# Bringing together the degrees' partial sums: two hops of small DMAs and a VectorE reduction in place of a TensorE matmul

## The reference

```
# layer 0: the same adj with x and with x2, an MLP of three ReLU layers on each
ax  = adj @ x          ; h = ax + (1 + eps) * ax ; 3 times: h = relu(h @ W[i].T + b[i])
x   = layernorm(x + concat(out1, out2) @ Wm.T + bm)
# layer 1: normalised by degrees
A_hat = adj + eye ; deg = sum(A_hat, axis=1) ; d = where(deg > 0, rsqrt(deg), 0)
x   = layernorm(x + (d[:, None] * A_hat * d[None, :] @ x) @ W.T + b)
```

## Time and profile before

| | |
|---|---|
| median of 3 runs | 594.1 us |
| the profiled execution | 593.58 us, of which span 591.8 us |
| TensorE matmul busy | 584.8 us (99%) |
| VectorE busy | 540.5 us (91%) |
| ScalarE busy | 372.2 us (63%) |
| GpSimd busy | 28.7 us (5%) |
| granted TensorE clock, mean | 0.997 |
| DMA, mean over the span | 239 GB/s |

### The profile page before, as it was taken

One profiled execution on the slowest core, in us unless ns is written; L12 is line 12 of the kernel. 1 busy time (PEld: TensorE's weight loads), 2 busy tenths in 40 slices (PEclk: granted clock), 3 DMA queues, 4 the chain that ended last, 5 costly groups with the idle time before them and its releaser, 6 DMA issues.

```text
span 591.8 us, 7721 instructions
## 1 busy us (share of the span) xinstructions
PE 584.8 (99%) x2676; PEld 484.3 (82%) x2676; DVE 540.5 (91%) x679; ACT 372.2 (63%) x494; POOL 28.7 (5%) x31
## 2 busy tenths in 40 slices
PE   8999999999999999999999999999999999999996
PEld 7888888888888888888888888867888888888885
DVE  6999999997988998998799999994899999989986
ACT  6554446842544773454667336486897888898893
POOL 1000000001100000110000020000200010010011
PEclk9999999999999999999999999999999999999998
DMA  9978565443554533354443375776699999999911
GB/s 334 370 271 296 202 226 197 142 148 137 214 205 170 190 145 142 142 213 174 181 150 138 138 293 189 286 299 212 245 353 413 364 370 383 400 365 374 387 42 71
DMA packets 27849, 141.56 MB, mean 239 GB/s; under 512 B 2608, under 2 KB 3376, under 8 KB 13616
## 3 DMA queue, kind: packets, MB, share of 16 engines
q1 hardware_dynamic: 27248, 139.54, 63.6%
q10 hardware_dynamic: 576, 1.70, 0.7%
HBM read 139.14 MB, written 2.10 MB: 239 GB/s over the span
## 4 chain that ended last, share of the span: by engine, by line
PE 98%; issue 0%; DVE 0%; POOL 0%; POOLq 0%; DVEq 0%
PE ps L468 81%; PE ps L544 7%; PE pd L486 6%; PE pd L497 2%; PE pd L530 1%; PE pd L592 1%; POOLq L118 0%; POOL rstd L1119 0%; DVE z L1090 0%; PE pd L494 0%; DVE stats L1095 0%; DVE outn L1104 0%; POOL identity L1123 0%; DVE mv L897 0%; DVEq L118 0%
## 5 line engine op out<-in xcount | busy, mean ns | idle before, releaser
L649 ACT ACTIVATE ahi<-raw 128x1024 fp32r<-128x1024 f32 x212 | 221.7, 1057 | 165.4 <-PE ps L468 152.8
L816 DVE TENSOR_TENSOR alo<-raw,ahi 128x1024 fp32r<-128x1024 f32 x212 | 257.2, 1220 | 29.7 <-ACT ahi L649 27.9
L468 PE MATMUL ps<-ahi,x2s 128*128 128x512 f32 x512 | 138.4, 389 | 0.0
L468 PE MATMUL ps<-ahi,x1hi 128*128 128x512 f32 x384 | 121.8, 393 | 0.0
L468 PE MATMUL ps<-alo,x1hi 128*128 128x512 f32 x384 | 120.5, 390 | 0.0
L468 PE MATMUL ps<-ahi,x1lo 128*128 128x512 f32 x384 | 120.4, 389 | 0.0
L468 PEld LDWEIGHTS ps<-ahi,x2s 128*128 128x128 f32 x512 | 96.1, 188 | 20.0
L468 PEld LDWEIGHTS ps<-ahi,x1hi 128*128 128x128 f32 x384 | 71.9, 188 | 15.9 <-issue 1.4
L468 PEld LDWEIGHTS ps<-alo,x1hi 128*128 128x128 f32 x384 | 72.0, 188 | 15.2 <-DVE alo L816 0.3
L468 PEld LDWEIGHTS ps<-ahi,x1lo 128*128 128x128 f32 x384 | 72.1, 188 | 14.9
L468 PE MATMUL ps<-alo,x2s 128*128 128x512 f32 x256 | 80.3, 389 | 0.0
(11 more groups left out here) (98 smaller groups left out, 510.7 us busy)
## 6 DMA issues: line engine op xcount, KB each, us to landing
raw<-a_t SPq DMA_DIRECT2D x108, 1024.0 KB, 4.9
raw<-a_t SPq DMA_DIRECT2D x32, 512.0 KB, 7.4
raw<-early SPq DMA_DIRECT2D x7, 512.0 KB, 7.8
xn<-x SPq DMA_DIRECT2D x3, 1024.0 KB, 8.1
out<-outn ACTq DMA_DIRECT2D x3, 512.0 KB, 6.7
par<-params SPq DMA_DIRECT2D x1, 708.0 KB, 12.8
raw<-head SPq DMA_DIRECT2D x2, 256.0 KB, 3.2
xn<-x SPq DMA_DIRECT2D x1, 512.0 KB, 7.2
```

Of the source, the lines that this page charges most:

```text
L468: mm = pe.matmul(ps[bank + (CH * (q % 2) if layer else 0)][:, :], block_of(w, n), a[c], start=(n == 0 and k == 0), stop=(n == JB - 1 and k ...
L649: act.activation(ring_hi(layer, q, n), raw_tile(layer, n), ACT.Copy).then_inc(hi_ready, 1)
L816: dve.tensor_tensor(ring_lo(layer, q, n), raw_tile(layer, n), as_f32(ring_hi(layer, q, n)), ALU.subtract).then_inc(lo_ready, 1)
```

## The change

`same_place`, `totals` and the matmul of `merge` go, with TensorE's waits for `partial_ready` and `deg_ready`. ScalarE gets two new steps in its order: `spread_partial` at n = 7 (plan 0) or 6 (plan 1) waits for `partial` and issues one DMA that writes it to DRAM (16 KB, 128 runs of 128 B); `gather_partial` two tiles later waits for that write and issues four DMAs that each read all four groups back to 32 partitions (16 KB, 128 runs of 128 B each). Both stand behind ScalarE's round of that tile and ahead of its ReLUs. VectorE's `degrees` waits for the four reads, adds the groups with one reduction and goes on as before, from SBUF.

```diff
--- before.py
+++ after.py
@@ -82,6 +82,7 @@
 DVE_AGGREGATE = (DVE_RESIDUAL[0] + 1 + KB // STATISTICS[0], DVE_RESIDUAL[1])
 DVE_DEGREES = tuple(k + 1 for k in DVE_RESIDUAL)
 DVE_TURN = (5, 4)
+ACT_SPREAD = (7, 6)
 DVE_BASE = 10
 DVE_BASE_LAST = 20
 DVE_SHIFT = tuple(k + 2 for k in DVE_AGGREGATE)
@@ -114,7 +115,7 @@
 X_AFTER = {1: 1, 3: 2, 6: 3, 12: 4, 20: 5}
 
 
-def build(nc, a_t, head, early, x12, params, out):
+def build(nc, a_t, head, early, x12, params, scratch, out):
     with ExitStack() as ctx:
         def sb(name, shape, dt=F32):
             return ctx.enter_context(nc.sbuf_tensor(name, shape, dt))
@@ -146,10 +147,11 @@
         hhi = sb("hhi", [P, M, CW], F32R)
         rowsum_all = sb("rowsum_all", [P, QW])
         partial = sb("partial", [P, QW // TB])
+        regrouped = sb("regrouped", [P, GROUPS, QW // TB])
+        together = sb("together", [P, QW // TB])
         own = sb("own", [P, QW // TB])
         degree = sb("degree", [P, KB])
         my_group = sb("my_group", [P, QW // TB])
-        same_place = sb("same_place", [P, P])
         xb = sb("xb", [P, KB, P])
         z = sb("z", [P, KB, P])
         par = sb("par", [P, PARAMS])
@@ -176,8 +178,6 @@
         merged = pd[:, 0:2, :].rearrange("p c (k d) -> p (c k) d", d=P)
 
         merged_last = lambda k: pd[:, 1 + max(k + 1 - TAIL[2][0], 0), (k % 4) * P:(k % 4 + 1) * P] if k >= HB else merged[:, k, :]
-        totals = pd[:, 2, 0:QW // TB]
-
         params_in = sem("params_in")
         x_in = [sem(f"x_in{i}") for i in range(len(X_PIECES))]
         x2_in = sem("x2_in")
@@ -206,6 +206,9 @@
         xb_ready = sem("xb_ready")
         turned_ready = sem("turned_ready")
         partial_ready = sem("partial_ready")
+        scratch_written = sem("scratch_written")
+        regrouped_in = sem("regrouped_in")
+        together_ready = sem("together_ready")
         own_ready = sem("own_ready")
         degree_ready = sem("degree_ready")
         deg_ready = sem("deg_ready")
@@ -490,8 +493,6 @@
             def merge(q):
 
                 wait(pe, h_ready, q * (4 * M) + 4 * M)
-                wait(pe, partial_ready, q + 1)
-                pe.matmul(totals, same_place[:, :], partial[:, :], start=True, stop=True, skip_group_check=True)
                 for k in range(KB):
                     for b in range(2):
                         mm = pe.matmul(merged[:, k, :], h[:, CH * b + k // 4, (k % 4) * P:(k % 4 + 1) * P],
@@ -505,7 +506,6 @@
                     if n == min(PE_DENSE[plan]):
                         wait(pe, raw_used, q * PAIRS + PAIRS)
                         wait(pe, z_ready, q)
-                        wait(pe, deg_ready, 2 * q)
                     dense(q, PE_DENSE[plan][n], plan)
                 if n == PE_MERGE[plan]:
                     merge(q)
@@ -684,6 +684,10 @@
             def mlp_step(q, n, plan):
                 if n == ACT_EVACUATE[plan]:
                     evacuate(q)
+                if n == ACT_SPREAD[plan]:
+                    spread_partial(q)
+                if n == ACT_SPREAD[plan] + 2:
+                    gather_partial(q)
                 if plan == 0 and n in (ACT_EVACUATE[0] + 1, ACT_EVACUATE[0] + 2):
                     for m in range(CH):
                         round_h(q, 0, CH * (n - ACT_EVACUATE[0] - 1) + m)
@@ -696,6 +700,18 @@
                     else:
                         to = lambda k: xn[:, bass.ds(q, 1), k * P:(k + 1) * P].rearrange("p o d -> p (o d)")
                     normalise(q + 1, to, xn_ready, range(size * (n - at), size * (n - at + 1)))
+
+            def spread_partial(q):
+
+                wait(act, partial_ready, q + 1)
+                act.dma_start(scratch, partial[:, :]).then_inc(scratch_written, 16)
+
+            def gather_partial(q):
+
+                wait(act, scratch_written, q * 16 + 16)
+                source = scratch.rearrange("(g r) b -> r g b", g=GROUPS)
+                for to in range(GROUPS):
+                    act.dma_start(regrouped[to * TB:(to + 1) * TB, :, :], source).then_inc(regrouped_in, 16)
 
             def round_y(g):
 
@@ -866,7 +882,11 @@
 
             def degrees(q):
 
-                dve.tensor_tensor(own[:, :], totals, my_group[:, :], ALU.mult).then_inc(own_ready, 1)
+                wait(dve, regrouped_in, (q + 1) * (16 * GROUPS))
+                dve.tensor_reduce(together[:, :], regrouped[:, :, :].rearrange("p g b -> p b g"),
+                                  mybir.AxisListType.X, ALU.add).then_inc(together_ready, 1)
+                wait(dve, together_ready, q + 1)
+                dve.tensor_tensor(own[:, :], together[:, :], my_group[:, :], ALU.mult).then_inc(own_ready, 1)
                 wait(dve, own_ready, q + 1)
                 dve.tensor_reduce(degree[:, :], own[:, :].rearrange("p (k g) -> p k g", g=GROUPS),
                                   mybir.AxisListType.X, ALU.add).then_inc(degree_ready, 1)
@@ -1124,14 +1144,8 @@
                                base=0, pattern=[[-1, P]], channel_multiplier=1).then_inc(warm_ready, 1)
             pool.wait_ge(warm_ready, 1)
             pool.memset(halves[:, :], -0.5).then_inc(const_ready, 2)
-            pool.memset(same_place[:, :], 0.0).then_inc(const_step, 1)
             pool.memset(my_group[:, :], 0.0).then_inc(const_step, 1)
-            pool.wait_ge(const_step, 3)
-            place = same_place[:, :].rearrange("p (g c) -> p g c", c=TB)
-            for g in range(GROUPS):
-                pool.affine_select(out=place, in_=place, compare_op=ALU.not_equal, fill=1.0, base=-TB * g,
-                                   pattern=[[0, GROUPS], [-1, TB]], channel_multiplier=1).then_inc(const_step, 1)
-                pool.wait_ge(const_step, g + 4)
+            pool.wait_ge(const_step, 2)
             of_group = my_group[:, :].rearrange("p (k g) -> p k g", g=GROUPS)
             for g in range(GROUPS):
                 pool.memset(of_group[g * TB:(g + 1) * TB, :, g], 1.0).then_inc(const_ready, 1)
@@ -1183,7 +1197,8 @@
     }
     nc = bacc.Bacc("TRN2", target_bir_lowering=False, num_devices=1)
     aps = [nc.dram_tensor(k, v.shape, F32, kind="ExternalInput").ap() for k, v in arrays.items()]
+    scratch = nc.dram_tensor("scratch", (P, QW // TB), F32).ap()
     out = nc.dram_tensor("out", (QUARTERS, P, QW), F32, kind="ExternalOutput").ap()
-    build(nc, *aps, out)
+    build(nc, *aps, scratch, out)
     r = run_bass_kernel_spmd(nc, [arrays], core_ids=[0])
     return r.results[0]["out"].reshape(_OUT)
```

## The result

| | before | changed |
|---|---|---|
| median of 5 runs each, us | 594.39 (594.02 to 594.75) | 603.17 (602.99 to 604.62) |
| ratio, 95% interval | | 1.0155 (1.0141 to 1.0169) |
| span of the profiled execution, us | 591.8 | 602.0 |
| mean granted clock | 0.997 | 0.996 |

The kernel became 8.8 us slower. 5.3 had been forecast, so the direction was right and the size was not: 603.2 lies above the range of 596.4 to 602.4.

A forecast was written before the change was run, and what follows sets the result against it. TensorE, busy 99% of the span, was taken to bound the kernel. The terms -0.56 + 3.0 + 2.6 + 0.3 = +5.3 us on the profiled 593.6 gave 598.9, as a median 599.4 us; range 596.4 to 602.4.

The forecast's parts named there:

- The matmul's 0.56 us: At the merges, removing the matmul of the degrees' totals frees TensorE of 0.14 us four times, 0.56 us less.
- VectorE's reduction: At the degrees, one added reduction of 0.29 us, some 0.35 with semaphore, four times; covered by idle time, at most 1.4.
- First layer, +3.0: ScalarE's wait for partial sums delays the ReLUs and last hlo; dense layer 1 stalls 1.0 us in three quarters.
- Rival (b): The first layer's stall does not show and only the second layer pays: 596.5 us, chance 0.11.
- Second layer, first stall, 2.6: Last quarter: ScalarE's wait and write issue delay the ReLUs; dense layer 1 has no room and stalls 2.6 us.
- catches up at its idle times near 129 to 138: First layer: VectorE falls up to 3 us back but recovers in its idle times at 129 to 138 us.
- Second layer, gather, 0.3: Before dense layer 2, the write lands in 4 us, four issues fit in the room; mean stall 0.3, ends 0 and 3.9.
- Rival (a): The write lands around 8 us in the second layer's busy stretch, 3.9 us of stall instead of 0.3: 603.0 us, chance 0.13.
- rival (d): TensorE's clock falls in the second layer's 2.6 us stall, up to 4.9 us more: up to 604.3, chance 0.04.
- Two of its own signs of being wrong: Among the listed signs: gaps lying at dense layer 2 or the merge, and the granted clock leaving 1.00.
- Rival (c): Waits are hidden because partial sums are ready before ScalarE comes; only 0.56 us counts: 593.5 us, chance 0.08.
- the estimate of 2.04 us: Landing time of the 16 KB write by the skill's fixed cost plus bytes; with it the gather waits for nothing.

The follow-up runs named there:

- e9: e1 with the new SBUF tiles laid out so that all other tiles keep their addresses from before the change; 593.77 us, ratio 0.9989 to before.
- e7: The kernel before plus only ScalarE's waits for the partial sums where the changed kernel has them, no DMAs; 600.50 us.
- e2: The changed kernel with ScalarE's DMA steps put behind the ReLUs in the first layer only; 600.35 us.
- e3: The changed kernel with ScalarE's DMA steps put behind the ReLUs in the second layer only; 597.79 us.
- e1: The changed kernel with ScalarE's DMA steps put behind the ReLUs of the same step in both layers; 594.46 us, ratio 1.0001 to before.
- e11: The changed kernel with the last quarter's write bringing only 16 of 128 partitions, the rest of those sums left out; 602.59 us.
- e5: The changed kernel with 14 extra matmuls, result unread, filling TensorE's pause ahead of the last quarter's dense layer 1; 604.93 us.
- e4: The changed kernel with the last quarter's four reads issued behind the ReLUs of layer 2; 602.38 us.
- e6: e4 with 14 extra matmuls, result unread, ahead of the last quarter's dense layer 1; 600.31 us.
- e10: The changed kernel with the write and four reads issued by GpSimd, ahead of its powers, instead of ScalarE; 594.54 us.
- e8: The kernel before plus five small DMAs a quarter at the same places on ScalarE, without the change's waits, data unused; 594.76 us.
- e12: e1 with 384 unused bytes a partition behind the new SBUF tiles, so later tiles lie 512 B higher than before; 593.90 us.

## Why the prediction was wrong, point by point

The step that failed is the price of the gather in the second layer, 0.3 us, where the runs show 2.74; a smaller one is the first stall there, 2.6, where they show 3.28. With the terms as measured the sum is 3.0 + 3.28 + 2.74 for the stalls, +0.72 for addresses and -0.80 - 0.16 for the matmul: 8.8 us.

- **The matmul's 0.56 us.** Too low for what TensorE is spared: 0.27 in the first layer and 0.35 in the second, each, and not the 0.14 of the chain's piece. The chain's piece of a pipelined pass is not what goes when the pass goes. And the premise that time leaves the kernel whenever TensorE has less to do failed in quarter 3, where VectorE, at 91% busy, took over the chain (e9).
- **VectorE's reduction.** 0.37 to 0.40 us, 0.29 forecast, covered nearly: in e9 VectorE's way from its reduction in quarter 3 to the last one is 0.06 us longer than before.
- **First layer, +3.0.** Right. Stretch A is 2.95 longer = -0.80 for the matmul, +0.72 for the addresses, +3.0 for the stalls, of which 2.9 stand at the dense layers 1 (1.11, 0.91 and 0.86 over 2.80). The place (dense layer 1, held by the last hlo), the mechanism and the size stand; the idle time is spread over the last two or three banks. e7 gave 2.05 for the wait alone where 2.0 came from the same rows. That the matmul and the addresses cancel so nearly is luck. Rival (b), no stall in the first layer, is refuted by this.
- **Second layer, first stall, 2.6.** The wait and the issue are right: 2.70. Too low is that VectorE's reduction was taken to stand where it stood; it came 0.58 later. The step that failed here is the sentence that VectorE "catches up at its idle times near 129 to 138". That holds in quarter 1. In quarter 3 it has further work (y for the second layer), shows no idle time before the second layer, and brought 0.3 us of its lateness (e2, e3) to the reduction for which ScalarE now waits. The other 0.3 is the matmul's gain of quarter 3, which TensorE has and VectorE hasn't (measured in e9; e1 and e2 show the same 0.3, and that it has the same cause there is argued from their chain and order, not tested).
- **Second layer, gather, 0.3.** Mis-sized by 2.4 us. The write took 6.2 us against 4 assumed and the four issues 2.57 against 1.5; that alone sets the 2.74 (e11 has 1.84 and e5 3.10 at full clock). Rival (a), a landing of 8 us, is this mechanism; that its 603.0 us comes so near to 603.2 is partly luck, since it put the write too late, and the issues and the first stall too low. The fall of the clock, rival (d), did happen, but under the wait for the write it cost nothing here; alone it costs 1.7 us (e4, e6, e7), not up to 4.9. The prediction had kept both as alternatives, each beside an otherwise kept forecast, and both came. Two of its own signs of being wrong, gaps at dense layer 2 and a clock that leaves 1.00, are in the profile.
- **Addresses.** Not thought of. +0.72 us, and by it the harmless version (e1) looks like no gain.
- **Rival (c)**, that the waits are hidden, is what e1 and e10 make true by another order. It fell as argued, by the 3.6 and 3.4 us in the earlier trace rows.

On the write, the Trainium skill ("DMA: Bandwidth & Descriptors", "Anatomy of one DMA") has about 2.0 us fixed for one DMA, a fit that its heading gives for the path of DMAs that GpSimd issues; this write was issued by ScalarE. The traces have 1.4 us with quiet engines and 4.6 to 6.8 with full ones, and for GpSimd's own write in e10 1.7 and 4.4; by the measurement the fixed part is no constant on either path, and the estimate of 2.04 us was wrong where it counted. On the clock its rule ("TensorE: Matmul & The Clock Gate", Part 1), that idle time brings the throttle back, was the better guide: after five of the six long pauses that nothing filled the clock fell, after e11's of 3.47 us it did not. I had set the rule aside by a row of the last microseconds.

## What to carry to other kernels

A wait put into an in-order engine costs what is queued behind it, so put it behind the work that the bounding engine is about to need: one wait a quarter, ahead of four ReLUs, cost 5.9 us here, and the same DMAs behind them, or on an engine with nothing to do, cost none. Before counting on work taken from the bounding engine, look at how far behind it the next one is: here VectorE took back 0.3 of 1.15 us. Price a pause of TensorE with the risk that the clock falls, and a small transfer by the traffic of its own moment, not by a quiet one. When tiles are added or dropped, look whether the others moved.

## What the runs showed of the hardware

- The granted clock fell to its half level (1.2 GHz) about when TensorE started again (between 0.3 us before, in e2 and e5, and 1.0 us after, in the changed kernel and e7) after it had been idle 3.53 us (changed), 3.50 (e4), 3.24 (e2), 3.15 (e5, at dense layer 2) and 2.62 (e7), and lasted through about one dense layer. After 3.47 us (e11) it stayed at 1.00. With the pause filled (e5, e6) it stayed at 1.00 through dense layer 1.
- A 16 KB write from SBUF to DRAM in 128 runs of 128 B landed 1.4 us after its issue at DMA shares of 0.07 to 0.25, and 4.6 to 6.8 us in the second layer's busy stretch (0.94 in the changed kernel).
- 128 B of shift in SBUF made a dense layer's twelve matmuls of 512 columns slower, 2.80 instead of 2.75 us on the chain (e1, e10 against e9); 512 B did not (e8, e12). Which operand's address does it was not tested.
- Four DMA issues in a row on ScalarE took 1.76 us in e9 and 2.57 in the changed kernel's second layer; the single one took 0.34 each time.
